# Output combinations of the last head pair placed at every third item of VectorE's program in place of every second

## What is computed

```python
xn = layernorm(x)
# s: attention of 16 heads of 64; the softmax runs over ALL keys, the causal mask is applied after it
Q, K, V = xn @ Wq, xn @ Wk, xn @ Wv
alpha = softmax(Q K^T / 8);  alpha = where(causal, alpha, 0);  s = alpha V
# g: one causal attention head of 128 whose projections are sums over gated experts (8 experts),
# and whose output goes through gated expert projections, then silu
g = silu(ffn(xn))
out = x + s * g
```

## Time and profile before

| | us |
|---|---|
| two timed runs | 3523.1 and 3631.6, median 3577.4 |
| profiled execution, time | 3515.8 |
| profiled execution, span of its slowest core (core 3) | 3514.2 |
| spans of the eight cores | 3496.9 to 3514.2 |
| last head pair, from VectorE's first instruction of it to the end | 402.5 |
| the pair before it | 307.3 |

### The profile page before, as it was taken

How to read it: one execution, slowest core, us unless ns; L and a number is a source line. 1 busy time by engine, 2 the same in 40 slices (tenths; PEclk the granted TensorE clock), 3 DMA queues, 4 the chain that set the end, 5 groups by cost and what they waited for, 6 DMA issues and landing times.

```text
span 3514.2 us, 59878 instructions; the slowest of 8 cores (3496.9 to 3514.2 us)
## 1 busy us (share of the span) xinstructions
PE 2553.1 (73%) x18642; PEld 1154.7 (33%) x18642; DVE 2273.6 (65%) x5890; ACT 2115.0 (60%) x2466; POOL 255.4 (7%) x706
## 2 busy tenths in 40 slices
PE   2179997675687777778777787887788887885651
PEld 1134443332233333333333333333333333332220
DVE  7447774233366776776677677667767766776764
ACT  0000003511177986897798689779868977996762
POOL 0100000000000000010000001000000100011012
PEclk9999999898878778768877876887787579655655
DMA  5510000113200000000000000000000000003346
GB/s 152 142 42 1 1 1 1 55 55 119 73 3 3 6 6 3 4 9 3 3 6 6 3 4 9 3 3 6 6 3 4 9 3 3 6 6 122 100 147 208
DMA packets 35776, 117.11 MB, mean 33 GB/s; under 512 B 5778, under 2 KB 5778, under 8 KB 35474
## 3 DMA queue, kind: packets, MB, share of 16 engines
q1 hardware_dynamic: 22738, 71.34, 6.2%
q0 software_dynamic: 12736, 41.95, 4.1%
HBM read 79.72 MB, written 33.55 MB: 32 GB/s over the span
## 4 chain that ended last, share of the span: by engine, by line
PE 32%; ACT 21%; DVE 18%; issue 16%; DMA 8%; DVEq 4%; POOL 0%; ACTq 0%; SPq 0%; POOLq 0%
ACT expC L1344 7%; ACT stagef L1359 6%; PE PB L889 5%; PE PB L903 5%; PE PB L874 5%; DVE cacc L1083 4%; PE PB L803 4%; PE PB L806 4%; PE PB L818 3%; PE PB L761 3%; ACT stagef L1344 3%; DMA stagef<-x 3%; ACT R L1359 3%; DVE tmpc L1207 3%; DVE stagef L1083 2%
## 5 line engine op out<-in xcount | busy, mean ns | idle before, releaser
L1207 DVE TENSOR_REDUCE tmpc<-stagef 128x2 f32<-128x1024 bf16 (+2 forms) x726 | 811.3, 1127 | 236.1 <-ACT stagef L1359 179.5
L1344 ACT ACTIVATE expC<-PB 128x1024 bf16<-128x1024 f32 x768 | 858.8, 1118 | 87.2 <-PE PB L889 87.2
L1359 ACT ACTIVATE stagef<-PB 128x1024 bf16<-128x1024 f32 x600 | 672.2, 1120 | 206.6 <-PE PB L903 131.4
L1207 DVE TENSOR_REDUCE tmpc<-R 128x2 f32<-128x1024 bf16 (+2 forms) x362 | 406.1, 1122 | 118.2 <-ACT R L1359 89.8
L1344 ACT ACTIVATE stagef<-PB 128x1024 bf16<-128x1024 f32 x384 | 432.2, 1126 | 73.5 <-PE PB L889 73.5
L889 PE MATMUL PB<-R 64*128 64x512 bf16 x1152 | 298.3, 506 | 234.3 <-ACT stagef L1359 138.0
L889 PE MATMUL PB<-QTt,KTt 64*128 64x512 bf16 x1152 | 285.4, 484 | 145.8 <-ACT stagef L1359 78.6
L1359 ACT ACTIVATE R<-PB 128x1024 bf16<-128x1024 f32 x296 | 332.0, 1122 | 83.8 <-PE PB L903 60.5
L683 PE MATMUL PB<-R,xnT 128*128 128x512 bf16 x1536 | 336.9, 379 | 2.4 <-DVE qk_tmp L1083 1.4
L1324 ACT ACTIVATE expC<-PB 128x512 bf16<-128x512 f32 x144 | 74.6, 611 | 364.8 <-PE PB L727 364.7
L903 PE MATMUL PB<-R 64*128 64x512 bf16 (+3 forms) x1088 | 263.2, 476 | 38.4 <-ACT expC L1344 19.6
(11 more groups left out here) (162 smaller groups left out, 2968.3 us busy)
## 6 DMA issues: line engine op xcount, KB each, us to landing
stagef<-x SPq DMA_DIRECT2D x64, 512.0 KB, 4.5
out<-Vau SPq DMA_DIRECT2D x32, 512.0 KB, 3.6
g_sp<-stagef SPq DMA_DIRECT2D x32, 256.0 KB, 2.0
s_sp<-s_stage POOLq DMA_DIRECT2D x64, 128.0 KB, 2.4
QTt<-g_sp POOLq DMA_DIRECT2D x32, 256.0 KB, 5.9
KTt<-s_sp POOLq DMA_DIRECT2D x32, 256.0 KB, 6.1
R<-qp POOLq DMA_DIRECT2D x8, 512.0 KB, 5.3
R<-kp POOLq DMA_DIRECT2D x8, 512.0 KB, 4.7
```

Source lines behind the costliest of these rows:

```text
L1207: e.tensor_reduce(s.tmpc[:].rearrange("p (h c) -> p h c", h=2)[:, :, c:c + 1], s.c1scr((m1 - 1) % 3)[:, 0:2 * kw] .rearrange("p (h k) -> p ...
L1344: e.activation(s.expCs(es), PB[[0, 1, 3][it["slot"]]][:, :], AF.Exp).then_inc(sem["aC2"], 1)
L1359: e.activation(scr[:, 0:1024], pbsrc[:, 0:1024], AF.Exp).then_inc(sem["aC1"], 1)
```

## The change

One number decides: a combination is taken off the list on every third call of `drip_cmb` in place of every second. The other lines rename nothing that runs (a local variable is written out, an unused semaphore is dropped, a blank line goes).

```diff
@@ names of semaphores
-            "tC2", "aC2", "gC2", "tU2", "vC2", "vC1r", "vM", "aRS", "gCM",
+            "tC2", "aC2", "gC2", "tU2", "vC2", "vC1r", "vM", "aRS",
@@ gpsimd_cmb_q
-            sl = k2 % 2
...
-            e.dma_start(s.QT[:, sl * 1024:sl * 1024 + 1024],
-                        gr[:, i, :]).then_inc(sem["dCG0" if sl == 0
+            e.dma_start(s.QT[:, (k2 % 2) * 1024:(k2 % 2) * 1024 + 1024],
+                        gr[:, i, :]).then_inc(sem["dCG0" if k2 % 2 == 0
@@ vector_p3
             def drip_cmb(force=False):
                 drip[0] += 1
-                if cmb_q and (force or drip[0] % 2 == 0):
+                if cmb_q and (force or drip[0] % 3 == 0):
                     self.vector_cmb_one(e, *cmb_q.pop(0))
```

More of the change, by code:

```diff
@@ L567, in gpsimd_cmb_q @@
             e.wait_ge(sem["dS30" if spar == 0 else "dS31"], scount)
-            e.dma_start(s.QT[:, sl * 1024:sl * 1024 + 1024],
-                        gr[:, i, :]).then_inc(sem["dCG0" if sl == 0
+            e.dma_start(s.QT[:, (k2 % 2) * 1024:(k2 % 2) * 1024 + 1024],
+                        gr[:, i, :]).then_inc(sem["dCG0" if k2 % 2 == 0
                                               else "dCG1"], 16)
-            e.dma_start(s.KT[:, sl * 1024:sl * 1024 + 1024],
-                        sr[:, i, :]).then_inc(sem["dCS0" if sl == 0
+            e.dma_start(s.KT[:, (k2 % 2) * 1024:(k2 % 2) * 1024 + 1024],
+                        sr[:, i, :]).then_inc(sem["dCS0" if k2 % 2 == 0
                                               else "dCS1"], 16)
```

## The result

| | before | changed |
|---|---|---|
| median of all timed runs | 3522.4 us (10 runs) | 3500.4 us (11 runs) |
| ratio, 95% interval | | 0.994, 0.9928 to 0.9952 |
| the same, measured a second time | | 0.9946, 0.9927 to 0.9965 |

The changed kernel is 19 to 21 us faster (0.5 to 0.6%). The forecast was 3502, by a gain of 18.3 us. The last pair takes 378.9 us on core 3 to the end of the span, where it took 402.5.

What follows compares the result with a forecast made beforehand. The prediction took the last pair's DMA waits on VectorE, passed to ScalarE, as the bound. Terms 4.7 + 7.2 + 5.0 - 0.4 + 4.1 - 2.3 = 18.3 us gave 3497.5 (profiled) or 3504.8 (timed); forecast 3502, range 3484 to 3560.

Steps and rivals of the forecast that it cites:

- slower rival: VectorE, not ScalarE, limits behind each group, so early reductions gain nothing and 7.9 us of delays remain: 3532; chance 10%.
- What bounds the kernel now: Last head pair: VectorE waits 98.4 us for combination loads, scratch tiles fill, ScalarE idles 70.0 us, TensorE stops behind it.
- A reduction in the wait is worth 1.81 us: Each reduction done while VectorE would stand still lets ScalarE do one more C1 and C2 pair, 1.81 us.
- Group 6, -4.7: Two more reductions ahead of the fourth combination (3.6 us), and the seventh reduction ends 1.1 us sooner: 4.7 us gained.
- Group 1, -4.1: Third and fourth combination move behind block 0's end; masks come 1.1 us later, yet block 0 ends 4.1 us sooner.
- Groups 4 and 3, -3.6 each: Two more reductions in the idle time, second combination not later: 3.6 us gained each, 7.2 in sum.
- Groups 5 and 2, -2.5 each: Two more reductions (3.6 us), but the second combination and the loads for the fourth come 1.1 us later: 2.5 gained each.
- group 7, +0.4: One reduction more (1.8 us) between first and second combination, with a tree; the fourth ends 2.25 us later: 0.4 lost.
- the fourth combination's 9.6 us may shrink: Second-to-fourth distance may fall to 8.5 where the second comes later: 1.1 us in four groups, 4.4 us; not counted.
- The tail, +2.3: Group 0's first combination, its x loaded late, starts 12.4 us after block 0's end begins, before 10.1: 2.3 lost.
- The waits fall by 10 to 15 us: Sign of being right: VectorE's waits ahead of the combinations' multiply (L543) fall that much from 98.4 us.
- GpSimd kept from its descriptors: Reductions beside GpSimd's loads delay them 1.13 us in each of six groups, 6.8 us: gain 11 us, about 3509; not counted.

Runs made afterwards that it cites:

- section 3: Changed kernel with a list of counts of reductions ahead of each combination in place of the counter; ratios to the kernel before from 1.0061 to 0.9845.
- 1, 0, 1, 0: Reductions ahead of each group's four combinations set to these counts, against 1, 1, 1, 1 before; ratio 1.0061, +21 us.
- 6, 4 and 3 alone: Every third item in these three groups only, every second in groups 7, 5, 2 and 1; ratio 0.9971 to the kernel before, -10 us.
- section 5: Changed kernel with x or g loads of group 0's first two combinations cut to 64 columns; first combination starts after 12.1 or 12.6 us, against 13.6.
- 5, 0, 5, 0: These counts of reductions ahead of the combinations in groups 7 to 3 (group 2: 4, 0, 4, 0; group 1: 3, 0); ratio 0.9845 to before, -55 us.

## Why the prediction was right

The gain and its mechanism were right: the sum is 18.3 us, measured 19 to 21, and the parts have the sign forecast, but for group 7's (+0.4 forecast, -0.4 measured). That 3502 lies so near the median of 3500.4 is in part luck, since it hangs on which execution the gain was taken from (3515.8 or 3523.1). The sizes inside the sum were off by up to 1.4 us and partly cancel. (The slower rival's 3532 is a slip: 3523.1 + 7.9 is 3531.)

*What bounds the kernel now.* The waits of the last pair for DMA, passed on to ScalarE by full scratch tiles: shown by the series of section 3, where time follows VectorE's wait ahead of L543. From 110.2 to 44.2 us of wait (66) the time goes from +21 to -55 (76).

*A reduction in the wait is worth 1.81 us.* Right as a mean, in both directions: 1.96 from 1, 0, 1, 0 to before, 1.63 and 1.89 for the next two steps, then 1.36. In the changed kernel itself it is 18.7 us for 11 reductions, 1.70 each. It isn't a constant: two reductions were worth 2.8 us in group 4 and 4.7 in group 5. In group 5 a tree moved ahead of the fourth combination too, which the ledger counted for group 6 alone.

*Group 6, -4.7*: measured -4.7, 3.7 for the two reductions and 1.1 for the fourth combination, as forecast.

*Group 1, -4.1*: measured -4.2, but by a path that the forecast had only in part. It had the masks end 1.1 us later and TensorE's last products bind the end of block 0. On core 3 the first mask comes 1.5 us later after the end of block 1, but the last mask ends 22.0 us after it in both kernels, and TensorE's last recorded product ends 1.2 us ahead of the end of block 0 (3451.45):

```profile
3449.31 0.54 POOL L511 TENSOR_SCALAR_AFFINE_SELECT mask<-stagef 128x128 bf16<-128x128 bf16 x2 [2.28 <-ACT stagef L1342]
...
3450.10 0.19 PE L863 MATMUL PB<-R,stagef 128*128 128x1 bf16 x1
```

What comes last is the last C1 item: VectorE waits 4.45 us for its exponential (3448.31), then reduces it and does the tree. It is so on all eight cores. So two errors of about a microsecond cancel in this term, and its good number is in part luck.

*Groups 4 and 3, -3.6 each*: -3.0 and -2.4. In group 4 the reductions were worth 2.8. In group 3 they were worth 3.2, and the distance from second to fourth grew from 11.3 to 12.3 us, which the forecast had constant, so the fourth came 0.7 later. In the kernel with 6, 4 and 3 alone that distance stayed at 11.2 and the piece gave -3.4; what shifted it in the whole change was not tried.

*Groups 5 and 2, -2.5 each, group 7, +0.4*: -3.9, -3.5, -0.4, each about 1 us better. These are the terms mis-sized, and not for one reason. In groups 7 and 2 it is the delay of the fourth combination. I had the bound "the fourth combination's 9.6 us may shrink" and took nothing of it. With two reductions between first and second the distance from second to fourth went from 11.7 to 10.3 in group 7 and from 11.9 to 10.6 in group 2, so the fourth came 0.9 us later in place of 2.25, and 0.5 sooner in place of 1.1 later. In group 5 that distance hardly moved (11.7 to 11.6), the fourth came 0.7 later, and the rest is the 4.7 us that its two reductions were worth. The shorter distances fit the crowd of transfers of section 5, since the loads now come further apart, but this was not tested.

*The tail, +2.3*: +3.1, and the reason was half right. x is issued late, as the prediction put it, but it isn't what the first combination waits for: that is the load of s, slowed by the traffic of x and the stores beside it.

*The waits fall by 10 to 15 us*: 20 as mean of the cores, 24.5 on core 3.

*GpSimd kept from its descriptors.* The upper bound of 6.8 us for loads held up by reductions beside them did not come in. The issues of loads in group 1 now, one with a reduction beside it (3440.30, VectorE's at 3439.62 and 3440.75):

```profile
3440.30 0.54 POOL L567 DMA_DIRECT2D QTt<-g_sp  x1 [4.63 <-DVE Vau L548]
...
3444.98 0.54 POOL L570 DMA_DIRECT2D KTt<-s_sp  x1
```

0.54 us, as before. The box of the Trainium skill (SBUF — State Buffer) speaks of operations in a two-port mode; whether the reduction is one no run here shows, and the 3509 took it for one without a reason. The measured gain of 19 to 21 us leaves that estimate's 11 outside its intervals.

## What to carry to other kernels

Where an engine with a fixed order waits for a transfer, count how much independent work stands ahead of the waiting instruction: "every n-th item" is a poor rule for that, and a list of counts fitted to each wait (5, 0, 5, 0 here) brought 55 us where the changed number brought 19. The worth of a filled wait is read at the pace of the engine that runs out of buffers (here 1.4 to 2.0 us as means for a reduction of 1.13), not from the filling work's own length. To check such a forecast, cut each stretch at the last instruction that waits for data: what lies behind it showed here to some 0.2 us what the moved work was worth, while the time of the whole is known to some 4 to 7. Waits for one of several rotating buffers are to be summed before they are compared.

## What the runs showed of the hardware

Transfers of one core that are issued together slow each other by much: the load of s (256 KB) lands in 4.1 us with 1.20 MB around it and in 8.8 us with 2.61 MB. With x issued ahead of the store on the same queue, x landed in 5.1 us in place of 5.4 and the store in 6.2 in place of 3.6 (medians, core 3), and the time showed no difference within 7 us. With the first two combinations 2.2 us apart in place of 3.0 (means of groups 7 to 2), the fourth came 12.0 us after the second in place of 11.6.

The eight cores do the same work in the last pair at different speed: from 390.3 to 400.5 us in one execution before the change. All of that spread lies in stretches with waits for transfers; from a group's fourth combination to the next end of block the cores agree to 0.15 us in that execution. It did not go with the waits filled: it is 373.4 to 376.4 in the profile of the changed kernel used here, but 369.9 to 383.4 in its first one, and 333.5 to 342.3 with 5, 0, 5, 0. Why one core's transfers take longer than another's was not tried.
